# Start-up of a fused attention and expert kernel: the first constants on ScalarE's queue, the norms ahead of the wait for them, residual rows ahead of the weight casts

## The reference

```
x = x + attn(layernorm(x))          # x: (2, 8192, 1024)
  Q, K, V = xn@W_q + b_q, xn@W_k + b_k, xn@W_v + b_v
  Q/32, K/32 and V are reshaped, not transposed: (2, 8192, 1024) -> (2, 16, 8192, 64)
  A = softmax(Q K^T)                # (2, 16, 8192, 8192)
  out = (diagonal(A)[..., None] * V).reshape(2, 8192, 1024) @ W_o + b_o
x = x + ffn(layernorm(x))
  expert = argmax(xn @ Wr.T + br)   # 8 experts
  y = W2[expert] @ relu(W1[expert] @ xn + b1[expert]) + b2[expert]
```

## Time and profile before

| what | us |
|---|---|
| median of 3 runs (2842.57 to 2848.65) | 2843.64 |
| the profiled execution's own time | 2841.02 |
| its span, core 0, the slowest (the fastest core: 2830.4) | 2839.3 |
| load of W_q issued | 1.73 |
| VectorE's first work on x | 25.29 |
| TensorE's first matmul (a turn of x) | 38.03 |
| first projection | 43.99 |
| first scores | 64.76 |
| first exponential on ScalarE | 67.14 |
| last exponential ends | about 2188 |
| experts' matmuls start | 2230 |

### The profile page before, as it was taken

One profiled execution on the slowest core, in us unless ns is written; L12 is line 12 of the kernel. 1 busy time (PEld: TensorE's weight loads), 2 busy tenths in 40 slices (PEclk: granted clock), 3 DMA queues, 4 the chain that ended last, 5 costly groups with the idle time before them and its releaser, 6 DMA issues.

```text
span 2839.3 us, 31237 instructions; the slowest of 8 cores (2830.4 to 2839.3 us)
## 1 busy us (share of the span) xinstructions
PE 2197.8 (77%) x10515; PEld 831.5 (29%) x10592; DVE 519.6 (18%) x1201; ACT 2158.7 (76%) x2721; POOL 144.9 (5%) x201
## 2 busy tenths in 40 slices
PE   3877677877776877778687877767676699999997
PEld 1222111211111212112111212101011477777775
DVE  3222111212111212221111211101010222222221
ACT  0999999999999999999999999999998111111110
POOL 0000000000000000000100000000000111110100
PEclk9787676768667675766676768555565799999998
DMA  9999999999999999999000000030000477777762
GB/s 186 142 108 117 122 121 120 122 119 113 118 122 123 119 118 123 114 119 115 13 19 1 19 1 19 8 122 12 1 12 0 165 255 261 251 247 257 251 242 73
DMA packets 38161, 324.54 MB, mean 114 GB/s; under 512 B 8784, under 2 KB 9680, under 8 KB 25712
## 3 DMA queue, kind: packets, MB, share of 16 engines
q0 software_dynamic: 16224, 157.39, 47.1%
q1 hardware_dynamic: 21776, 165.05, 16.8%
HBM read 443.70 MB, written 159.73 MB: 213 GB/s over the span
## 4 chain that ended last, share of the span: by engine, by line
ACT 47%; PE 37%; issue 13%; DVE 1%; DMA 1%; SPq 0%; POOL 0%; DVEq 0%; ACTq 0%; POOLq 0%
ACT EA L539 24%; ACT EB L539 23%; PE PS L498 10%; PE PS L510 10%; PE PS L421 9%; PE PS L262 4%; PE PS L377 1%; PE PS L283 1%; PE PS L472 1%; DMA GM<-c_gm 1%; PE PS L352 0%; PE PS L458 0%; DVE BN L586 0%; DMA out_t<-VB,PAD 0%; PE PS L367 0%
## 5 line engine op out<-in xcount | busy, mean ns | idle before, releaser
L421 PE MATMUL PS<-AR 64*128 64x512 bf16 x4096 | 1107.3, 526 | 518.1 <-ACT EA L539 291.2
L539 ACT ACTIVATE EA<-PS,NEGD 128x1536 bf16<-128x1536 f32 (+1 forms) x640 | 1122.5, 1754 | 22.8 <-PE PS L421 20.5
L539 ACT ACTIVATE EB<-PS,NEGD 128x1536 bf16<-128x1536 f32 x640 | 1012.9, 1583 | 25.5 <-PE PS L421 24.4
L421 PEld LDWEIGHTS PS<-AR 64*128 64x128 bf16 x4096 | 171.7, 99 | 1213.9 <-issue 1211.7
L262 PE MATMUL PS<-XLT,WR 128*128 128x512 bf16 x707 | 282.2, 482 | 18.8 <-issue 11.0
L551 ACT ACTIVATE AR<-PS,B1C 128x320 bf16<-128x320 f32 x128 | 67.5, 527 | 274.1 <-PE PS L498 227.9
L510 PE MATMUL PS<-AR,WR 128*128 128x320 bf16 x1664 | 229.9, 299 | 0.0
L498 PE MATMUL PS<-AR,WR 128*128 128x320 bf16 x1600 | 224.3, 301 | 1.0 <-DVE AR L788 1.0
L557 ACT ACTIVATE XR<-PS,B2C 128x320 f32<-128x320 f32 x32 | 16.9, 527 | 270.7 <-PE PS L510 270.7
L510 PEld LDWEIGHTS PS<-AR,WR 128*128 128x128 bf16 x1664 | 162.1, 98 | 61.9
L498 PEld LDWEIGHTS PS<-AR,WR 128*128 128x128 bf16 x1600 | 157.5, 98 | 62.5 <-issue 1.3
(11 more groups left out here) (101 smaller groups left out, 1032.1 us busy)
## 6 DMA issues: line engine op xcount, KB each, us to landing
w1b<-w1t POOLq DMA_DIRECT2D x64, 1024.0 KB, 19.2
w2b<-w2t POOLq DMA_DIRECT2D x64, 1024.0 KB
WR<-w2b SPq DMA_DIRECT2D x26, 2048.0 KB
WR<-w1b SPq DMA_DIRECT2D x25, 2048.0 KB
XA<-w1b SPq DMA_DIRECT2D x7, 2048.0 KB
XA<-w2b SPq DMA_DIRECT2D x6, 2048.0 KB
XA<-x SPq DMA_DIRECT2D x16, 512.0 KB, 54.7
XR<-x SPq DMA_DIRECT2D x16, 512.0 KB, 53.9
```

Of the source, the lines that this page charges most:

```text
L421: mm = e.matmul(PS[:, (n % 2) * 4 + i, :], kb[w % 2][hp:hp + 64, gb // 2, t0 * P:(t0 + 1) * P], QB[w % 2][hp:hp + 64, ga // 2, :], start=T ...
L539: e.activation(EO[n % 2][:, 0:size * 512], PS[:, b0:b0 + size, :].rearrange("p a b -> p (a b)"), AF.Exp, bias=NEGD[:, w % 2, t0, gb:gb + 1 ...
```

## The change

Four things, all in the start of the program:

1. The five `first_loads` are issued from ScalarE's queue, as the first things that it does, and no longer from SyncE's behind x.
2. VectorE does the moments, the scales and the norms of the first window, and reads the four turned tiles, before it waits for `sINA` and scales the biases.
3. SyncE waits for W_k, then loads the second window's x and the first residual rows, and only then the 16 `later_loads`. GpSimd, before its first cast of expert weights, waits for the residual rows and for `sINB` too.
4. The first chunk of K, its swapped copy and its diagonal move ahead of the last two chunks of Q: the order is Q0 to Q5, K0, Q6, swap, diagonal, Q7.

```diff
 (TensorE)
             e.wait_ge(sINA, N_INA)
-            for _ in chain(*[xlt(0, i) for i in range(4)], *[proj(0, 0, c) for c in range(DC)],
-                           proj(0, 1, 0), swap_k(0, 0), diag(0, 0)):
+            for _ in chain(*[xlt(0, i) for i in range(4)], *[proj(0, 0, c) for c in range(6)],
+                           proj(0, 1, 0), proj(0, 0, 6), swap_k(0, 0), diag(0, 0), proj(0, 0, 7)):
                 pass
 (ScalarE)
         def _(e):
+            for sb, srcap in first_loads:
+                e.dma_start(out=sb[:], in_=srcap).then_inc(sINA, 16)
             n = 0
 (VectorE)
             e.memset(ZERO[:], 0.0).then_inc(vI, 1)
-            e.wait_ge(sINA, N_INA)
-            step(e.tensor_scalar(BQS[:], BQS[:], SCALE, None, ALU.mult))
-            step(e.tensor_scalar(BKS[:], BKS[:], SCALE, None, ALU.mult))
             for tc in range(4):
                 tile_moments(0, tc)
...
             xlt(3)
-            for c in range(DC):
+            e.wait_ge(sINA, N_INA)
+            step(e.tensor_scalar(BQS[:], BQS[:], SCALE, None, ALU.mult))
+            step(e.tensor_scalar(BKS[:], BKS[:], SCALE, None, ALU.mult))
+            for c in range(6):
                 query(0, c)
             key(0, 0)
+            query(0, 6)
             swap_k(0, 0)
+            query(0, 7)
 (SyncE)
             load_xa(0)
-            for sb, srcap in first_loads:
-                e.dma_start(out=sb[:], in_=srcap).then_inc(sINA, 16)
+
+            e.wait_ge(sW[1], 16)
+            load_xa(1)
+            for tc in range(4):
+                load_xr(0, tc)
             for sb, srcap in later_loads:
...
             e.wait_ge(sINB, N_INB)
             e.dma_start(out=idxd.rearrange("(p a) o -> p (a o)", p=P), in_=PAD[:]).then_inc(sPAD, 16)
-            load_xa(1)
-            for tc in range(4):
-                load_xr(0, tc)
 (GpSimd)
             e.wait_ge(sW[3], 16)
+            for tc in range(4):
+                e.wait_ge(sXR[tc], 16)
+            e.wait_ge(sINB, N_INB)
             for k in range(NE * 8):
```

## The result

The changed kernel takes 2825.36 us in the median of 4 runs (2823.83 to 2830.98), the kernel before 2843.93 beside it (4 runs). The ratio is 0.9935, with a 95% interval of 0.9918 to 0.9953: 18.6 us faster, between 13 and 23. The forecast was 2826.5. The profiled execution took 2825.26, 15.8 less than that of before.

What follows compares the result with a forecast made beforehand. The prediction took the 67 us start, before ScalarE's and then TensorE's untouched work, as what could shrink: 16.1 + 0.95 = 17.05 us off 2843.64 gives 2826.6, forecast 2826.5, with 8 in 10 between 2821 and 2832.

Steps and rivals of the forecast that it cites:

- What bounds the kernel: From the first exponential, ScalarE's then TensorE's work, both untouched; only the start, 67 us with ScalarE idle, can shrink.
- Part 1, the norms: At the start, norms stop waiting for constants; x's fourth tile releases the first turn at 21.9, 16.1 us earlier.
- far bound of 9.9 us: Largest delay of x's fourth tile, if all five first constants pass before it; 0.8 us was taken.
- VectorE's chain: At the start, fourth tile's moments to first norm take 5.85 us, then 0.96 more to the first turn.
- The constants: The five first constants, on ScalarE's queue beside x, land at about 17 to 18, four us before the turn.
- Rival (a): At the start, constants land no earlier, at 24.5, and hold the turn to 24.7: gain 14.2, 2829.4 us; chance 0.10.
- Part 2, the order: Before the first scores, reordering Q and K chunks cuts TensorE's idle time: 0.95 us saved, at worst 0.8 lost.
- W_k: K's weights land at about 39, or 39.8 with x's delay; K's first chunk doesn't wait, at worst 1.4 us.
- Part 3: SyncE's loads queued behind W_k cost nothing: later constants land by 114.5, router sums need them at about 130.
- The sum: First scores and end come 16.1 + 0.95 = 17.05 us earlier, giving 2826.6 us, forecast as 2826.5.
- The clock in the stage behind: From 67 to 190, TensorE's slow clock could save or cost 3 us; taken as 0; faster rival 2823.5, chance 0.08.

Runs made afterwards that it cites:

- queue_only: Kernel before with only the five first constants moved to ScalarE's queue, VectorE still waiting for them before the moments; ratio 0.9985 (0.9948 to 1.0021).
- order_only_2: Kernel before with only K's first chunk, swap and diagonal moved between the last chunks of Q, a repeat on an undisturbed die; ratio 0.9992.
- const_first_sp: Changed kernel with the five first constants on SyncE's queue in front of x instead of on ScalarE's; ratio 0.9974 to the kernel before.
- x_first: Changed kernel with an early small exponential on ScalarE and W_q's cast held until x's third tile landed; ratio 0.9925 to the kernel before.
- norms_only: Kernel before with only VectorE's norms moved ahead of its wait for the constants, which stay behind x on SyncE's queue; ratio 0.9950.
- table_warm: Changed kernel with an early small exponential on ScalarE and 84 matmuls on zeros on TensorE before the first turn; ratio 0.9927 to the kernel before.
- the second comparison: The changed kernel run once more, unaltered, against the kernel before on the same chip; ratio 0.9927 (0.9912 to 0.9942).
- no_hold: Changed kernel whose expert weight casts start once W_o has landed, without waiting for residual rows and later constants; one run, 2825.82 us.
- no_sp_order: Changed kernel with later constants directly behind x on SyncE's queue and no further waits before the expert casts; ratio 0.9935 to the kernel before.

## Why the prediction was right

- **What bounds the kernel.** Right. The start moved and the stages behind it didn't. Median of the cores: first scores 16.2 us earlier, first exponential 16.4, router sums 15.9, last exponential 15.7. The stage behind gave back some 0.7 us, which is within its scatter.
- **Part 1, the norms.** Right in mechanism: the turn is released by the fourth tile's chain (22.69 on core 0, forecast 21.9), and 15.3 us were gained, forecast 16.1. Two sizes were short. The fourth tile came 1.2 us late where I took 0.8. Up to 19 us ScalarE's queue carried 720 packets, 45 for each DMA engine and not 40, at 0.014 us each (3.4% of 16 x 19 us) and not 0.025: their own time comes to 0.65 us, and the rest of the 1.2 is open. The prediction's far bound of 9.9 us should read 10.3 by its own two times (14.2 and 24.5).
- **VectorE's chain**, the second short size. From the start of the fourth tile's moments to the norm it took 6.21 us in place of 5.85. Of its 13 small steps, each 0.16 or 0.17 before, one took 0.50 and one 0.36; a pause of 0.53 before a later step became 0.38. That isn't chance, nor the traffic of that moment: the chain takes 5.83 to 5.86 us on every core of the kernels in which VectorE waits for the constants first (before, queue_only, order_only_2), and 6.19 to 6.22 on every core of those in which it waits for the fourth tile, even in const_first_sp, where it starts at 25.03. In x_first, without that wait, it takes 5.7 to 6.2. So it goes with the order of edit 2; why, no run shows.
- **The constants.** Forecast to land at 17 to 18, landed at 18.5. norms_only and queue_only show the two halves apart: 13.6 and 6.0 us at the first scores, against 16.2 for all four edits. They don't add up, since both lift one and the same wait and the later of two landings decides. Rival (a), the constant as the next bound, is what is left if only the norms are moved.
- **Part 2, the order.** Forecast 0.95, measured 1.11 on core 0 (8.42 us from Q5's read to the scores, now 7.31) and 1.1 by itself. Of that 0.85 is idle time saved (1.96 to 1.11), the rest closer following of the matmuls. A term was missing beside it: how long the projections run at the slow clock isn't fixed. On core 0 the six chunks of Q took 13.45 us to the read of the last in place of 12.35, which took the gain of the order back. That is largely the draw of one core: the 8 cores of the kernel before take 12.2 to 13.5 us (median 12.65), those of the changed kernel the same range (medians 13.37 and 12.99). That it is the clock shows in the matmuls, 0.43 us each at first and 0.21 later, and in core 1 of table_warm, where after the dummies seven chunks run in 12.4 us.
- **W_k.** It landed at 38.2 (forecast 39 to 39.8) and K0 didn't wait. But the price of not having edit 3 was mis-sized: I held 41.5, that of before, for the worst, and it is 44.2 with three queues at work, 5.0 us of waiting on core 0 and a chunk at half speed behind it. queue_only says why: edit 1 by itself puts W_k 2.7 us later. I had booked edit 3 at nothing and its help to W_k inside part 2 at 2.5 us; at the first scores it is worth 4.1 us, at the end nothing that shows.
- **Part 3.** Right: `sINB` was complete at 82 (bound 114.5), 49 us before the router sums; the casts began at 82.4 and ended at 1326.9 plus a landing, far ahead of their readers.
- **The sum.** On core 0: 15.34 for the turn, -1.10 for the clock, +1.11 for the order, 15.36 at the first scores with rounding, 15.6 at the end of the span; forecast 17.05. So the sum was 1.7 us too large, and that the forecast of 2826.5 lies only 1.1 us from the measured median is in part luck. That the median of the runs moved by 18.6 is within its interval of 13 to 23 and no evidence for the larger sum: the second comparison gave 20.8 us by its ratio (16 to 25), the profiled executions 15.8.
- **The clock in the stage behind** was left at zero, and the runs show nothing beyond its scatter, which is the noise on everything here. From the first exponential to the router sums, single cores of one profile take 75.5 to 80.0 us (kernel before), and no_hold and the changed kernel, with the same TensorE program, take 77.1 and 79.4 in the median of their cores. A start that is 1 us better can't be followed to the end in one profile.

## What to carry to other kernels

When an engine waits for several things at the start, list for each wait which instruction behind it first reads the data, and order the engine's program by what lands first. A small constant behind a large load costs little in bytes and much in rounds: its packets take turns with whatever else the DMA engines carry, so give it a queue of its own, neither behind nor in front of the large load. And when a start is shortened, look at once for the next landing (here W_k), because moving work up moves its demand for weights up too, and loads that move up with it (here the later constants) make those weights later.

## What the runs showed of the hardware

- Five small loads (73 KB) in front of x on the same queue delayed x's first tile by 8.8 us and the fourth by 9.5; on another queue they delayed the fourth by 1.2 (core 0 of each kernel).
- The table load of 1.28 us can be done at 3.7 to 4.4 us, in ScalarE's idle time, by an exponential of 8 columns, and doesn't come again at the first real one.
- Matmuls on a tile of zeros raise TensorE's clock too: on the slowest core the later turns behind them take 0.61 us for eight matmuls in place of 1.01, and its first projections run at 2.4 GHz (64 matmuls of 512 columns in 13.97 us), where in the changed kernel they began at 1.2 (0.43 us each). On the other seven cores the clock was lost again before or in the projections.
- The profile's granted clock reads 1.00 from 28.6 to 34.5 in the changed kernel, though the matmuls there take 0.43 us each and 0.21 from then on. So the level at the start is read off the matmuls here. After 5 us of waiting for W_k in no_sp_order it does show, as 0.57, and the next chunk takes twice its time.
